# First and last block of a cross-network contraction split over both halves of TensorE, and the chains at both ends rewritten

## The reference

```python
# x0: (B=2048, M=32 fields, D=16), gathered from 32 tables by ids
xk = x0
for W in (W0, W1, W2):                   # W0 (32,32,64), W1 and W2 (32,64,64)
    xk = relu(einsum('bmd,bhd,mhk->bkd', x0, xk, W))
    outs.append(sum(xk, axis=2))         # over d
z = concatenate(outs, axis=1)            # (2048, 192)
h = concatenate([z, dense_ctx], axis=1)  # (2048, 208)
h = maximum(h @ W_top1 + b_top1, 0)      # 512
h = maximum(h @ W_top2 + b_top2, 0)      # 256
y = h @ W_top3                           # (2048, 1)
```

## Time and profile before

| what | value |
|---|---|
| median of three runs | 1333.74 us (1332.66 to 1334.31) |
| the profiled execution's own time | 1334.63 us |
| its span in the trace | 1332.4 us |
| TensorE matmul busy | 1248.2 us, 94% |
| VectorE busy | 1157.5 us, 87% |
| GpSimd busy | 645.2 us, 48% |
| ScalarE busy | 502.9 us, 38% |
| mean granted TensorE clock | 0.992 |

### The profile page before, as it was taken

The page is one execution under the profiler, slowest core; times in us unless marked ns, Lnnn a source line. Parts: engine busy times, 40 slices in busy tenths (PEclk is TensorE's granted clock), DMA queues, the critical chain, the costliest instruction groups (busy, mean ns, idle before and its releaser), DMA issues.

```text
span 1332.4 us, 15126 instructions
## 1 busy us (share of the span) xinstructions
PE 1248.2 (94%) x5696; PEld 433.7 (33%) x5696; DVE 1157.5 (87%) x534; ACT 502.9 (38%) x728; POOL 645.2 (48%) x676
## 2 busy tenths in 40 slices
PE   0399999999999999999999999999999999999995
PEld 0133333333333333333333333333333333333343
DVE  2159999999999999999999999899999989899971
ACT  0234344433443443334343443444344334434310
POOL 6777665545454664445466544545665451111111
PEclk9999999999999999999999999999999999999997
DMA  5499888898989877778888978788899987778710
GB/s 113 103 255 241 234 226 249 223 232 230 234 228 241 224 223 227 203 223 227 248 240 221 230 221 220 209 229 234 226 227 222 232 231 224 203 223 236 211 29 1
DMA packets 74423, 281.53 MB, mean 211 GB/s; under 512 B 30103, under 2 KB 38986, under 8 KB 41550
## 3 DMA queue, kind: packets, MB, share of 16 engines
q1 hardware_dynamic: 57666, 275.35, 74.9%
q0 software_dynamic: 16384, 4.23, 3.3%
q10 hardware_dynamic: 300, 0.99, 0.3%
HBM read 276.28 MB, written 4.20 MB: 211 GB/s over the span
## 4 chain that ended last, share of the span: by engine, by line
PE 79%; DVE 8%; issue 5%; ACT 5%; POOL 2%; DMA 0%; POOLq 0%; ACTq 0%; DVEq 0%
PE accs L498 58%; PE acc L487 9%; DVE prod L443 7%; PE wide L477 5%; ACT sq L321 3%; PE exch L509 2%; POOL emb L225 2%; PE exch L518 2%; PE wide L469 1%; ACT parts L305 1%; DVE parts L433 1%; ACT xp L341 0%; ACT xp L340 0%; PE exch L528 0%; PE wide L518 0%
## 5 line engine op out<-in xcount | busy, mean ns | idle before, releaser
L443 DVE TENSOR_TENSOR prod<-kept,xp 128x2048 f32<-128x2048 f32 x512 | 1135.1, 2281 | 109.7 <-ACT xp L341 42.6
L498 PE MATMUL accs<-prod,w2s 128*64 128x512 f32 x2048 | 962.7, 599 | 8.1 <-DVE prod L443 8.1
L498 PE MATMUL accs<-prod,w1s 128*64 128x512 f32 x2048 | 953.1, 598 | 3.7 <-DVE prod L443 3.7
L225 POOL DMA_INDIRECT emb<-in_tbl,idx x512 | 484.7, 947 | 153.1 <-issue 145.6
L498 PEld LDWEIGHTS accs<-prod,w1s 128*64 128x64 f32 x2048 | 264.0, 137 | 466.1 <-issue 455.6
L498 PEld LDWEIGHTS accs<-prod,w2s 128*64 128x64 f32 x2048 | 259.6, 137 | 75.0 <-issue 42.1
L321 ACT ACTIVATE sq<-wide 128x1024 f32<-128x1024 f32 x160 | 163.9, 1024 | 278.7 <-PE acc L487 247.4
L254 POOL TENSOR_TENSOR x3f<-x3f 64x512 f32<-64x512 f32 x32 | 40.7, 1271 | 438.2 <-ACT x3f L350 438.2
L487 PE MATMUL acc<-sq,u 128*64 128x512 f32 x640 | 173.6, 599 | 0.2 <-ACT sq L321 0.2
L477 PE MATMUL wide<-x,sums 64*128 64x512 f32 x320 | 81.1, 504 | 11.1 <-ACT sq L321 10.4
L350 ACT ACTIVATE x3f<-accs 64x512 f32<-64x512 f32 x64 | 38.0, 593 | 115.8 <-PE accs L498 115.0
(11 more groups left out here) (37 smaller groups left out, 366.0 us busy)
## 6 DMA issues: line engine op xcount, KB each, us to landing
kept<-x_rows SPq DMA_DIRECT2D x256, 512.0 KB, 4.4
kept<-x_rows SPq DMA_DIRECT2D x512, 256.0 KB, 5.2
emb<-in_tbl,idx POOLq DMA_INDIRECT x512
x_rows<-x3f SPq DMA_DIRECT2D x32, 128.0 KB
prod<-in_w_all ACTq DMA_DIRECT2D x1, 512.0 KB, 6.5
w1s<-in_L_rec_W SPq DMA_DIRECT2D x4, 128.0 KB, 3.6
w2s<-in_L_rec_W SPq DMA_DIRECT2D x4, 128.0 KB, 3.5
wt<-in_W_top SPq DMA_DIRECT2D x1, 512.0 KB
```

Source lines behind the costliest of these rows:

```text
L225: pool.indirect_dma_start(emb[t % 2][:, m, :], None, tables[m], bass.IndirectOffsetOnAxis(ap=idx[:, t, m:m + 1].bitcast(U32), axis=0)).the ...
L443: nc.vector.tensor_tensor(prod[layer][:, q % BUFS[layer], :, :], kept[:, q % KEPT, :, :], xp[layer][:, :].unsqueeze(1).to_broadcast([128, ...
L498: last = mm(accs[64 * (layer - 1):64 * layer, s % 2, :], wk[layer][:, t, :], prod[layer][:, q % BUFS[layer], i, :], start=t == 0, stop=t = ...
```

## The change

It has these parts.

- `halved(layer, s)` is true for block 0 of layer 1 and block 63 of layer 2. There `contract` issues two matmuls of 256 columns with the same weights, the first half of the columns into partitions 0 to 63 of the bank and the second into 64 to 127. `take_x2` and `take_x3` copy from both places, in twice as many instructions of half the width. TensorE waits, before the first contraction of blocks 0 and 63 of layer 2, until x2 of the same block has been taken.
- The high and low parts of the first tile are made in two halves of d each; the first `turn` waits for the first halves only.
- The field rows of the first pair are copied in two parts, one by ScalarE and one by VectorE; `store_fields(0)` waits for these two and not for the square.
- The groups are 4, 4, 4, 3 and 1 tiles. The nine pieces of the group of three stand at n = 248 to 256.
- The z3 sums of the last tile: GpSimd adds blocks 60 to 62 and folds them to 128 columns; VectorE folds block 63 twice and adds the two.
- The last y is computed as a row of one partition and 128 columns, copied to `y_last` and stored from there as one row.

```diff
-GROUPS = [(0, 4), (4, 4), (8, 4), (12, 2), (14, 1), (15, 1)]
+GROUPS = [(0, 4), (4, 4), (8, 4), (12, 3), (15, 1)]
...
-            elif g == 3:
-                at[start + 2 + 2 * q, 2] = (g, q)
             else:
-                at[start + 3 + q // 3, 1 + q % 3] = (g, q)
+                at[start - 7 + q, 2] = (g, q)
...
+HALF = BLK // 2
+def halved(layer, s):
+    return (layer, s) in ((1, 0), (2, BLOCKS - 1))
...
             def store_fields(p):
-                sp.wait_ge(s_took, 6 * p + 2)
+                if p == 0:
+                    sp.wait_ge(s_fields0, 1)
+                    sp.wait_ge(s_first0, 1)
+                else:
+                    sp.wait_ge(s_took, 6 * p + 2)
...
+                else:
+                    sp.wait_ge(s_taken, 7 * g + 4)
+                    sp.dma_start(out.rearrange("b one -> one b")[:, first * NB:B], y_last[:, :]).then_inc(s_out, 16)
...
+            def z3_last_but_one():
+                pool.wait_ge(s_z3p, PAIRS - 1)
+                pool.wait_ge(s_xz[3], BLOCKS - 1)
+                pool.tensor_tensor(x3[:, 0, :], x3[:, 0, :], x3[:, 2, :], ALU.add).then_inc(s_z3t, 1)
+                pool.wait_ge(s_z3t, 2 * BT - 1)
+                pool.tensor_tensor(x3[:, 0, 0:2 * NB], x3[:, 0, 0:2 * NB], x3[:, 0, 2 * NB:4 * NB],
+                                   ALU.add).then_inc(s_z3t, 1)
+                pool.wait_ge(s_z3t, 2 * BT)
+                pool.tensor_tensor(x3[:, 0, 0:NB], x3[:, 0, 0:NB], x3[:, 0, NB:2 * NB], ALU.add).then_inc(s_z3t, 1)
...
+            def split_first_high():
+                act.wait_ge(s_gather[0], 16 * M)
+                for half, signal in ((slice(0, D // 2), s_high0), (slice(D // 2, D), s_high)):
+                    nc.scalar.copy(parts[:, half, 0, :], emb[0][:, :, half].rearrange("p m d -> p d m"))\
+                        .then_inc(signal, 1)
...
-                if t == 0:
-                    if p:
-                        act.wait_ge(s_stored, 16 * p)
+                if t == 0 and p == 0:
+                    nc.scalar.copy(fields[:, 0, :], wide[0:M, 0, :]).then_inc(s_first0, 1)
+                    act.wait_ge(s_fields0, 1)
+                elif t == 0:
+                    act.wait_ge(s_stored, 16 * p)
                     nc.scalar.copy(fields, wide[0:M, :, :])
...
-                src = accs[0:64, s % 2, :]
-                nc.scalar.activation(xp[2][0:64, :], src, ACT.Relu)
-                nc.scalar.activation(xp[2][64:128, :], src, ACT.Relu).then_inc(s_x[2], 1)
+                if halved(1, s):
+                    src = [(accs[64 * c:64 * c + 64, s % 2, 0:HALF], slice(HALF * c, HALF * c + HALF))
+                           for c in range(2)]
+                else:
+                    src = [(accs[0:64, s % 2, :], slice(0, BLK))]
+                for half in range(2):
+                    for bank, cols in src:
+                        last = nc.scalar.activation(xp[2][64 * half:64 * half + 64, cols], bank, ACT.Relu)
+                last.then_inc(s_x[2], 1)
...
-                    nc.scalar.copy(y[:, BT - 1:BT], exch[:, 0:1]).then_inc(s_taken, 1)
+                    nc.scalar.copy(y_last[:, :], exch[0:1, 0:NB]).then_inc(s_taken, 1)
...
+            def z3_last():
+                dve.wait_ge(s_xz[3], BLOCKS)
+                nc.vector.tensor_tensor(x3[:, 3, 0:2 * NB], x3[:, 3, 0:2 * NB], x3[:, 3, 2 * NB:4 * NB],
+                                        ALU.add).then_inc(s_z3l, 1)
+                dve.wait_ge(s_z3l, 1)
+                nc.vector.tensor_tensor(x3[:, 3, 0:NB], x3[:, 3, 0:NB], x3[:, 3, NB:2 * NB],
+                                        ALU.add).then_inc(s_z3l, 1)
+                dve.wait_ge(s_z3l, 2)
+                dve.wait_ge(s_z3t, 2 * BT + 1)
...
+                nc.vector.tensor_tensor(z3d[0:K, g % 2, 0:NB], x3[:, 3, 0:NB], x3[:, 0, 0:NB],
+                                        ALU.add).then_inc(s_z3, 1)
...
-            split_low(0)
+            split_first_low()
+
+            dve.wait_ge(s_wide, 2)
+            nc.vector.tensor_copy(fields[:, 1, :], wide[0:M, 1, :]).then_inc(s_fields0, 1)
...
-                if p % 2 == 0:
+                if p == 0:
+                    pe.wait_ge(s_low0, 1)
+                else:
                     pe.wait_ge(s_low, p // 2 + 1)
-                if p:
...
-                last = mm(accs[64 * (layer - 1):64 * layer, s % 2, :], wk[layer][:, t, :],
-                          prod[layer][:, q % BUFS[layer], i, :], start=t == 0, stop=t == 15)
+                if t == 0 and (layer, s) in ((2, 0), (2, BLOCKS - 1)):
+
+                    pe.wait_ge(s_xz[2], s + 1)
+                if halved(layer, s):
+                    for c in range(2):
+                        last = mm(accs[64 * c:64 * c + 64, s % 2, 0:HALF], wk[layer][:, t, :],
+                                  prod[layer][:, q % BUFS[layer], i, HALF * c:HALF * c + HALF],
+                                  start=t == 0, stop=t == 15)
+                else:
...
-            y_rows(g).then_inc(s_ev, 1)
+            for k in range(2):
+                last = mm(exch[0:1, 0:NB], wt3[:, k:k + 1], h2[:, k, 0:NB], start=k == 0, stop=k == 1)
+            last.then_inc(s_ev, 1)
```

More of the change, by code:

```diff
@@ L142, in tower @@
         s_took = sem("wide_taken")
+        s_high0 = sem("first_high_ready")
+        s_low0 = sem("first_low_ready")
+        s_first0 = sem("first_block_fields_copied")
+        s_fields0 = sem("second_block_fields_copied")
         s_l0 = sem("l0_tile_done")
@@ L200, in store_y @@
                 first, tiles = GROUPS[g]
-                sp.wait_ge(s_taken, 7 * g + (7 if g < LAST_GROUP else 4))
-                sp.dma_start(out.rearrange("(t p) one -> p (t one)", p=NB)[:, first:first + tiles],
-                             y[:, first:first + tiles], allow_slow_non_contiguous=True).then_inc(s_out, 16)
+                if g < LAST_GROUP:
+                    sp.wait_ge(s_taken, 7 * g + 7)
+                    sp.dma_start(out.rearrange("(t p) one -> p (t one)", p=NB)[:, first:first + tiles],
+                                 y[:, first:first + tiles], allow_slow_non_contiguous=True).then_inc(s_out, 16)
+                else:
+                    sp.wait_ge(s_taken, 7 * g + 4)
+                    sp.dma_start(out.rearrange("b one -> one b")[:, first * NB:B], y_last[:, :]).then_inc(s_out, 16)
             store_fields(0)
@@ L284, in _ @@
                     z12_fold(s // 4)
-                if s > 0 and (s - 1) % 2:
+                if s > 0 and (s - 1) % 2 and s < BLOCKS:
                     z3_pair((s - 1) // 2)
-                if s > 0 and (s - 1) % 4 == 3:
+                if s > 0 and (s - 1) % 4 == 3 and s < BLOCKS:
                     z3_fold((s - 1) // 4)
+            z3_last_but_one()
         @block.scalar
@@ L349, in take_x3 @@
                     act.wait_ge(s_z3, s // 4)
-                nc.scalar.activation(x3[:, s % 4, :], accs[64:128, s % 2, :], ACT.Relu).then_inc(s_xz[3], 1)
+                if halved(2, s):
+                    for c in range(2):
+                        last = nc.scalar.activation(x3[:, s % 4, HALF * c:HALF * c + HALF],
+                                                    accs[64 * c:64 * c + 64, s % 2, 0:HALF], ACT.Relu)
+                else:
+                    last = nc.scalar.activation(x3[:, s % 4, :], accs[64:128, s % 2, :], ACT.Relu)
+                last.then_inc(s_xz[3], 1)
             def take_event(g, e):
@@ L429, in _, with split_first_low @@
                 .then_inc(s_u, 1)
+            def split_first_low():
+                for half, ready, signal in ((slice(0, D // 2), s_high0, s_low0), (slice(D // 2, D), s_high, s_low)):
+                    dve.wait_ge(ready, 1)
+                    nc.vector.tensor_tensor(parts[:, half, 1, :], emb[0][:, :, half].rearrange("p m d -> p d m"),
+                                            parts[:, half, 0, :].bitcast(FP32), ALU.subtract).then_inc(signal, 1)
+            def z3_last():
[7 more added lines that the diff above has]
+                dve.wait_ge(s_z3t, 2 * BT + 1)
+                g = LAST_GROUP
+                dve.wait_ge(s_ev, 7 * (g - 2) + 4)
+                dve.wait_ge(s_z3, BT - 1)
+                nc.vector.tensor_tensor(z3d[0:K, g % 2, 0:NB], x3[:, 3, 0:NB], x3[:, 0, 0:NB],
+                                        ALU.add).then_inc(s_z3, 1)
             def split_low(t):
@@ L454, in _ @@
                     split_low(n // 16 + 1)
+            z3_last()
         @block.tensor
@@ L497, in contract @@
                     pe.wait_ge(s_xz[layer + 1], s - 1)
-                last = mm(accs[64 * (layer - 1):64 * layer, s % 2, :], wk[layer][:, t, :],
-                          prod[layer][:, q % BUFS[layer], i, :], start=t == 0, stop=t == 15)
+                if t == 0 and (layer, s) in ((2, 0), (2, BLOCKS - 1)):
+                    pe.wait_ge(s_xz[2], s + 1)
+                if halved(layer, s):
+                    for c in range(2):
```

(6 more changed lines are left out.)

8 lines of the change are left out of this document (6 added, 2 removed).

## The result

The changed kernel takes 1315.72 us (median of four runs, 1313.77 to 1317.1), beside 1333.2 us for the kernel before (1332.28 to 1334.31). The ratio is 0.9867, with a 95% interval of 0.985 to 0.9885. That is 17.5 us less, where 24 to 25 were forecast; the time lies inside the range (1305.5 to 1316.5), near its upper end. The profiled execution took 1315.46 us, its span is 1313.6 us.

A forecast was written before the change was run, and what follows sets the result against it. VectorE's products and TensorE's contractions were both nearly full, neither alone setting the pace, so the gain lies at the two ends: 5.5 + 11.3 + 3.7 + 4.7 - 0.1 = 25.1 off 1334.6, so 1309.5 us; range 1305.5 to 1316.5.

The forecast's parts named there:

- The first chain: Start of the kernel: halved conversions let TensorE begin 0.85 us earlier, x1 comes 1.1 us earlier; bounds 0.6 to 1.6 us.
- The start, the halved block 0: Layer 1's units 0 to 3 cost 6.9 us, not 13.8; product (2,0) at 88.2, -5.5 us (range -2.5 to -6.3).
- rival (b): Start gives little: rows or squares hold TensorE, or the half clock lasts; gain 2, time 1313.0; chance 0.17.
- The regrouping: Units 241 to 255: -2.3 us from pieces gone, +2.5 at 248 to 255; end of 255 moves to about 1286.2.
- Layer 2 alone: Last contractions, VectorE the bound in units 253 to 255: unit 255 ends at 1302.5, not 1311.2, -8.7 us.
- Tail: Sums before h1, three adds on VectorE: h1 starts 2.1 us after the last contraction, not 4.6, -2.6 us.
- The clock: In h1 and h2 TensorE's full level stays: 1.85 us each, -3.7 over both.
- rival (a): The clock falls in the tail: 1313.6; chance 0.20.
- The store: End of the kernel: last y stored as one contiguous row in 2.0 us, -4.7 us after the copy.
- The bound drawn through the two landings: Last store: 256 elements land in 9.2, 128 in 6.8, zero pieces at 4.4, so the gain would be 2.4.
- The case of a row cut into small pieces: Last store: transfers under 512 B pay a read-modify-write; a cut row would make the sum 2.3 us worse.
- rival (d): Slower: VectorE's 110 us of waits around the body's products grow; at 26% the time is 1338; chance 0.02.

## Why the prediction came out as it did

**The first chain** held as far as it goes. TensorE's first transposes came at 46.57 (46.8 forecast), the store was issued at 49.98 (50.25), and x1 was ready for the products 1.8 us before its old time (product 0 starts at 61.73, before at 63.52), where 1.1 were forecast. No run undoes this part by itself.

**The start, the halved block 0** is the step that failed: -5.5 forecast, 1.25 at product (2,0) and nothing that stands out from the scatter at the end of the body. The part on TensorE held: unit 3 was done at 81.0 and unit 5 at 91.0, where the prediction has 79.6 and 89.6, and before they were at 87.8 and later. The 1.4 us between prediction and trace come from x1 of block 1, which waited for the late product 3. Two terms of the sum did not hold:
- The rows were priced at the old rate (3.8 us a unit from 67.1 on, the eighth at 86.1). The products that wait for them start 4.2 to 5.4 us apart, and the eighth and the store behind it were through at 90.7. That the changed start would keep the old rate was taken over, and no row stood behind it.
- The landing of the last gather was priced at 2.36 us, from the first tile, when the queues were empty. With kept rows in the queues it took 7.3 (issued at 83.0, landed at 90.3), and 5.1 already in the kernel before, where the same working would have given 90.9 for product (2,0) and not 88.2. Through ScalarE's order this held x2, as the experiment with the later high parts shows: without it product (2,0) is 4.2 us earlier.

Late rows were in the text, as the lower side of the range (-2.5) and in rival (b) with 0.17 (gain 2). The late gather was not: the text takes the gathers as fixed, "in nobody's change", and rival (b) has only rows, squares and the clock. The gain was smaller than even (b) allows.

What makes the rows slower is not settled. It goes with the start as changed, for it showed in all four executions with it that are free of the long waits and in neither without. It is not the halving of block 0 (231 GB/s without it), nor the place of the high parts (249). What is left is the two-part conversion, the two-part copy of the fields, and the store issued 2 to 3 us earlier. A kernel with the old wait on the square for the first store would have told the last apart; it was not tried.

**The regrouping.** The end of layer 1 moved by +0.8 us relative to the body, as forecast (71.3 to 72.1). With the single tile's pieces gone from the stretch alone, the whole step is worth 2.4 us by its own experiment, 3.2 with a wait for rows that came in there; its 2.6 was about right.

**Layer 2 alone**: 16.3 us forecast, 16.46 measured. VectorE set the pace of block 63 as worked out; units 253 to 255 start 2.2 us apart. Taken alone, the halving gives 5.0.

**Tail**: 2.1 forecast from the last contraction to h1, 2.04 measured, where it was 4.75. That VectorE makes the last sums has no experiment of its own; the chain shows its three adds (0.43, 0.29 and 0.29 us) in the place of GpSimd's four. That is what the prediction took (0.42, 0.28, 0.28), though the one row it names, 477 ns for 320 columns, can't give both a fixed part and a price per column.

**The clock**: rival (a) came true in the profiled execution, partly. (The prediction reads the fall of before as 2.8 us after TensorE had stopped; the trace has it at 1314.2, 3.0 us after.) h1 gave back 1.3, h2 nothing. The forecast 1.85 for each is 1.99 where the clock stays. The prediction took it that the full level stays, and its chances of 0.55 and 0.20 were too far apart; the executions since say about even. The rule of the Trainium skill ("TensorE: Matmul & The Clock Gate", Why this matters for your kernels) is that idle gaps between bursts of matmuls, if long enough, send the clock back to half. These rows neither bear it out nor refute it: behind 2.04 us of idle before h1 (1.86 in one) the clock fell in five of nine executions, and did not in four.

**The store** gave 5.8 us, not 4.7: the forecast 2.5 us after the copy were 1.5. The bound drawn through the two landings of 128 and 256 elements left at most 2.4 and was far off. The case of a row cut into small pieces did not arise, for the trace has it as one packet of 512 bytes.

The sum again, with what was measured: start 0 to 1.2 (5.5), regrouping and stretch alone 9.2 - 0.8 = 8.4 and h1's earlier start 2.7, together 11.1 (11.3), clock 1.3 (3.7), store 5.8 and y -0.7 (4.7 and -0.1). That makes 17.5 to 18.8. So 4.3 to 5.5 us of the difference are the start, 3.0 the clock (2.4, and 0.6 of y's), and 1.1 came back from the store. The mechanism of the end was right and that of the start was not; that the time still lies inside the range is owed to its width and to a store that was priced too carefully.

## What to carry to other kernels

When a stage is sped up, price the next transfers at what they will meet, not at what the trace shows from an emptier moment: here a gather that landed in 2.4 us on empty queues took 5.1 beside bulk loads before the change and 7.3 after it, and an in-order engine handed that wait to work that did not need the gather. Put work whose input may be late behind work whose input is there, and undo each part of a change by itself: block 0's halving looked like the mirror image of block 63's, and one was worth 1 us at most, the other 5. At the end of a kernel, a last result stored as one contiguous row rather than as one element per partition was worth about 6 us by itself.

## What the runs showed that was not expected

- The first eight units of kept rows moved at 281 and 284 GB/s in the kernel before and at 231 to 250 with the changed start, with the queues 102 to 103% busy in all. The bytes are the same, so each took longer. The cause is open.
- The body, from the fifth pair of blocks on, repeats to 0.05 us a pair from one execution to the next (36.29, 37.91, 39.99 and so on, by the pair's place), with or without the change, so a shift at the start stands until the end. This is why rival (d) had no ground.
- TensorE's clock fell or stayed with the same idle of 2.04 us before h1 and the same instructions in h1: it fell early in h1 (3.64 us), late in it (2.39 us), or not at all (1.99 us).
- From the copy of y to the end of the span the column's store took 7.3, 8.0 and 8.3 us in three executions, the row's 1.5 in eleven.
- The gather whose landing took 2.4 us on empty queues took 5.1 to 5.2 beside the kept rows in the kernel before, and 7.3 to 8.7 in the four executions with the changed start.
